# A graph network on one core: both RGCN tables made in one block, tiles posted by ACT, fewer waits and shorter register rows on TensorE, and the clone rows made inside the first dense product

## The chip, the core and the metric

The kernel runs on one core of a Trainium2 chip. The metric is the device time of one execution in microseconds, the median of several. The engines are named as in the profile: PE (TensorE; its weight loads are PEld), DVE (VectorE), ACT (ScalarE), POOL (GpSimd) and SP (SyncE). A trailing q (PEldq, POOLq, SPq) means the sequencer of an engine: register loads, semaphore posts, branches and the issue of DMAs.

## The reference

There are N = 3125 nodes with 128 features and 50,000 edges (src, dst), sorted by dst; each edge has one of R = 9 types. Four graph layers follow each other, each with a residual and a layer norm:

```
x = layernorm(x + ARMA(x))        # two stacks of 3, dense products with D^-1/2 A D^-1/2
x = layernorm(x + GCN(x))
x = layernorm(x + RGCN(x))        # two layers, below
x = layernorm(x + sum over edges of x[src] @ W_neigh.T + b + x @ W_self.T + b)
```

The RGCN, which matters here, has in each of its two layers 18 weights and biases (9 types, two directions) and one for the node itself. With cnt[s] the number of edges of kind s at a node (at least 1):

```
hidden = output @ W[-1] + b[-1]
for r in range(R):
    for inv in (0, 1):
        s = r + R * inv
        msum = agg[s] @ W[s] + count[s] * b[s]     # agg[s]: sum of output over edges of kind s
        hidden = 2.0 * (hidden + msum) / cnt[s]
```

Unrolled, every edge adds to its node one row, output[other end] @ W[s] + b[s], times a factor that depends on the node and the kind; the own row has a factor as well.

## The kernel before

The nodes are NT = 25 tiles of P = 128. The program is a row of stages. Each stage opens a block in which every engine has its own instruction list, and a barrier of all engines stands between two blocks (in the profile the lines L801, L1447, L1549 and the like are such boundaries). The order of work inside a block is written out by hand, with semaphores.

Stages, in order of time: loading, sorting of the edges by either end and counting (to 645 us); `heavy_stage`, which finds nodes of unusually many edges ("clones": a node's second row) and the list `k.need`; `staircase_stage` and `pair_counts_stage`, which make the dense matrix of edge counts (`pairs`, 25 tiles of 128 x 3200 in fp16, and `exact` in uint16) and end at 895 us; `clone_rows_stage` (L1544), to 910; the first dense product `sum_x` in `dense_stage`; the ARMA layers; GCN; and then, for each RGCN layer, two table stages, the sum and a turn back; at last the neighbour layer.

**`clone_rows_stage`.** POOL gathers 128 rows of `exact` and 128 of `pairs` (L1560, L1561), DVE subtracts (L1566), SP stores the difference behind the last real rows of `pairs` (L1571): counts that don't fit fp16 go in two parts.

**`dense_stage`.** SP streams tiles of `pairs` through a ring of four (L1652). DVE, ACT split the features in bf16 parts (L1745, L1777, L1780), PE multiplies (L1694), 21 matmuls a tile. `beside` is other work that DVE does behind its splits; `loads` are weights for later that SP issues between tiles. POOL copies rows out (L1628).

**`table_stage`.** For a layer it makes first `by_src`, then `by_dst`: for every node and type the row output @ W[s] + b[s], 9 x 128 floats, in DRAM. ACT copies a tile of the transposed features into `fed` (L878), PE does three 128x384 products of it (L869; PSUM banks in a ring of J = 5), DVE adds the bias and drains each (L895), SP stores the tile (L935) from a ring of five. SP also waits for stores: `landed(t - BACK)` with BACK = 2 posts tile t - 2 into `tiled` (L929), after it has issued the store of tile t. POOL waits in `behind` for `tiled` to reach `needs[n]` (L2558) and gathers the first BEHIND = 48 rows lists (L2546: 128 edges each, one indirect DMA of 128 rows of 512 bytes) into the ring `got` of PLACES = 128. `needs` is in integer registers from `k.need`, computed in `heavy_stage` as the row number times 1/1152 plus 1.01, rounded, at most NT. In the second table stage POOL gathers 56 more, up to EARLY = 104, and PE and DVE make the own row of each node, in seven groups of four tiles (L827, L837, L841).

**`typed_sum_stage`.** It works in steps of U = 16 items. An item is 128 edges of one order and one node tile: POOL has gathered the 128 rows (L2099; a POOL wait for `ps_sum_rgcn L2180` means that the ring is full), SP posts landed groups of four (L2080), DVE has made a 128 x 128 selection `select` with the edges' factors (L2255), and PE multiplies the two into the PSUM slot of the node tile (L2180). There are C = 416 items an order, 832 a layer, so 52 steps. In layer 0 the factors are found on the way (`find`): for later steps PE also turns one-hots (L2108 `flip`) and looks up the factors (L2115 `look`), DVE copies (L2232), chooses (L2236 to L2248), closes the selection (L2255) and makes the next one-hot (L2227, which posts `heated`). For each half step (OCTET = 8 items) the PE sequencer loads 8 x 4 registers from `k.ring` (L2155): PSUM slot, `freed` count, place in `got`, `landed` count; in layer 0 it also loads 8 of `look_at` (L2123). At the top of a step it waits for `heated` and `selected`. ACT empties and seeds PSUM slots (L2218, L2203), reading where a tile ends from five-register loads (L2211).

Of the kernel before, what the change touches and what calls it, by code (L numbers as in the profile page):

```python
# [16 lines left out]
P = 128  # L17
# [761 lines left out]
BACK = 2  # L779


def piece(first, width, terms, bias=None, target=None):

    return first, width, terms, bias, target


def table_stage(nc, k, tag, pieces, tables, width, scale=None, gathers=None, behind=None, own=None):  # L790
# [10 lines left out]
    with Stage(nc, tag) as c:  # L801
# [8 lines left out]
        if own is not None:  # L810
            own_weights, own_xT, own_bias, own_factor, own_acc = own
            ps_own = c.psum("ps_own", [P, 8 - J, 512])
            own_multiplied, own_biased, own_scaled = c.sems("own_multiplied", "own_biased", "own_scaled")
        FOURS = -(-NT // 4)

        def four(g):

            return slice(4 * g, min(4 * g + 4, NT))

        def own_product():  # L820

            for g in range(FOURS):
                tiles = four(g)
                if g >= 8 - J:
                    nc.tensor.wait_ge(own_biased, g - (8 - J) + 1)
                for t in range(tiles.start, tiles.stop):
                    last = nc.tensor.matmul(ps_own[:, g % (8 - J), t % 4 * P:t % 4 * P + P], own_xT[:, t * P:t * P + P],  # L827
                                            own_weights, start=True, stop=True)
                last.then_inc(own_multiplied, 1)

        def own_sum():

            for g in range(FOURS):
                tiles = four(g)
                n = tiles.stop - tiles.start
                nc.vector.wait_ge(own_multiplied, g + 1)
                nc.vector.tensor_tensor(own_acc[:, tiles, :],  # L837
                                        ps_own[:, g % (8 - J), 0:n * P].rearrange("p (t f) -> p t f", f=P),
                                        own_bias[:, None, :].to_broadcast([P, n, P]), ALU.add).then_inc(own_biased, 1)
                nc.vector.wait_ge(own_biased, g + 1)  # L840
                nc.vector.tensor_tensor(own_acc[:, tiles, :], own_acc[:, tiles, :],  # L841
                                        own_factor[:, tiles, None].to_broadcast([P, n, P]), ALU.mult).then_inc(own_scaled, 1)

        if gathers is not None:
            @block.gpsimd
            def _(gp):
                gathers(gp)

        if behind is not None:
            (tiled,) = c.sems("tiled")  # L850

            @block.gpsimd
            def _(gp):
                behind(gp, tiled)

        @block.tensor
        def _(pe):
            nc.tensor.sem_inc(multiplied, M * J)
            if own is not None:
                own_product()  # L860
            with pe.Fori(0, TURNS) as i:
                for m in range(M * J):
                    j, (first, w, terms, bias, target) = m // M, pieces[m % M]
# [9 lines left out]
        def feed(engine, copy):  # L873
            with engine.Fori(0, TURNS) as i:
                for j in range(J):
                    engine.wait_ge(multiplied, i * (M * J) + M * j + M)
                    for q, turned in enumerate(feeds):
                        copy(fed[:, j, q, :], turned[:, bass.ds((i * J + j) * P, P)]).then_inc(copied, 1)  # L878

        def drain_turn(engine, i, first_turn):  # L880
            for m in range(M * J):
                j, (first, w, terms, bias, target) = m // M, pieces[m % M]
                if m % M == 0 and not first_turn:
# [1778 lines left out]
```

## Time and profile before

| what | value |
|---|---|
| time, median of 3 runs | 4873.02 us (4870.8 to 4875.13) |
| profiled execution | 4878.79 us, span 4877.5 us |
| granted TensorE clock, mean | 0.796 of full speed |
| adjacency to the end of the clone rows | 645 to 909.9 us |
| first dense product | 910 to 1025 us |
| tables, layer 0 and 1 | 2647 to 2802 us, 3699 to 3855 us |
| sum, layer 0 and 1 | 2802 to 3694 us, 3855 to 4706 us |

The span is the time from the first to the last instruction in the profile. Times in all views are counted from the start of the span. A timeline row gives the start, the duration (of a run of like instructions, from the first start to the last end), the engine, the line of the kernel, the instruction and its count, and in brackets how long the engine had been idle and what released it; "issue" there means that nothing shown in the profile held it.

### The profile page before, as it was taken

How to read it: one execution, taken by the hardware profiler on the slowest of the kernel's cores; microseconds unless marked ns; L12 is line 12 of the kernel's file. 1: busy time of each engine (PE TensorE's matmuls, PEld its weight loads, DVE VectorE, ACT ScalarE, POOL GpSimd, SP SyncE). 2: the span in 40 equal slices, each digit the busy share in tenths (PEclk: the TensorE clock that was granted, in tenths of full speed). 3: DMA queues.
4: the chain of work that ended last, by engine and by line, in shares of the span. 5: the costliest groups of instructions: out<-in, count | busy, mean ns of one | idle time of the engine just before them, and what ended most of it. 6: DMA issues, size and time to landing. Idle time of an engine off the chain costs nothing. (4 is left out here: it accounts for less than half of the span.)

```text
span 4877.5 us, 63370 instructions
## 1 busy us (share of the span) xinstructions
PE 3725.2 (76%) x16872; PEld 2405.0 (49%) x16874; DVE 2430.0 (50%) x3836; ACT 955.7 (20%) x2715; POOL 2043.5 (42%) x2229
## 2 busy tenths in 40 slices
PE   5977966698999979999989567676676665444459
PEld 2544522356555535555555356566564454333345
DVE  7988989405888861111235544444444633222221
ACT  2946838323000031111121000000001000000011
POOL 0000011103776611011101667777774777777740
PEclk7988979899999989999989755656667765555569
DMA  3000015715888817446544522222224422222224
GB/s 139 0 0 0 0 68 202 224 64 207 293 293 291 292 63 239 143 167 221 181 149 161 213 66 52 53 53 53 52 53 152 171 53 53 52 53 53 52 69 165
DMA packets 168584, 593.25 MB, mean 122 GB/s; under 512 B 47569, under 2 KB 59442, under 8 KB 168061
## 3 DMA queue, kind: packets, MB, share of 16 engines
q0 software_dynamic: 97200, 308.78, 20.7%
q1 hardware_dynamic: 70854, 282.16, 16.3%
q8 instruction: 69, 1.13, 0.1%
q14 instruction: 71, 0.57, 0.0%
q10 hardware_dynamic: 390, 0.60, 0.0%
HBM read 445.10 MB, written 146.27 MB: 121 GB/s over the span
## 5 line engine op out<-in xcount | busy, mean ns | idle before, releaser
L2180 PE MATMUL ps_sum_rgcn<-gathered_rgcn,select_sum_rgcn 128*128 x3328 | 1010.3, 450 | 446.1 <-SPq L2080 241.9
L2180 PEld LDWEIGHTS ps_sum_rgcn<-gathered_rgcn,select_sum_rgcn 128*128 128x128 f32 x3328 | 787.3, 306 | 525.5 <-issue 519.0
L2099 POOL DMA_INDIRECT gathered_rgcn<-by_dst,row x782 | 737.8, 944 | 238.3 <-issue 226.4
L2099 POOL DMA_INDIRECT gathered_rgcn<-by_src,row x574 | 541.6, 944 | 203.4 <-issue 160.6
L726 PE MATMUL ps_sum_arma<-gathered_sum_arma,select_sum_arma 128*128 128x384 f32 x1664 | 553.3, 492 | 20.3 <-DMA gathered_sum_arma<-arma,other 18.1
L712 POOL DMA_INDIRECT gathered_sum_arma<-arma,other x416 | 393.4, 946 | 382.3 <-POOLq L801 211.9
L1694 PE MATMUL ps_sum_arma<-pair_counts_sum_arma,parts_sum_arma 128*128 128x448 f16 x2625 | 519.5, 354 | 5.3 <-DMA pair_counts_sum_arma<-pairs 5.3
L726 PEld LDWEIGHTS ps_sum_arma<-gathered_sum_arma,select_sum_arma 128*128 128x128 f32 x1664 | 308.3, 191 | 265.1 <-issue 61.5
L760 DVE TENSOR_TENSOR acc_arma_end<-acc_arma_end,ps_sum_arma 128x768 f32 x416 | 396.9, 954 | 58.6 <-PE ps_sum_arma L726 36.2
L2108 PE MATMUL ps_turn_sum_rgcn<-ident,one_hot_sum_rgcn 128*128 128x128 bf16 x832 | 243.9, 301 | 232.8 <-issue 198.3
L2255 DVE TENSOR_TENSOR select_sum_rgcn<-one_hot_sum_rgcn,ps_coef_sum_rgcn 128x2048 f32<-128x2048 bf16 x52 | 119.0, 2288 | 584.3 <-PE ps_sum_rgcn L2180 584.2
L1694 PEld LDWEIGHTS ps_sum_arma<-pair_counts_sum_arma,parts_sum_arma 128*128 128x128 bf16 x2625 | 257.5, 98 | 226.7 <-DMA pair_counts_sum_arma<-pairs 5.8
L2218 ACT COPY acc_rgcn<-ps_sum_rgcn 128x128 f32<-128x128 f32 x100 | 26.5, 265 | 1686.2 <-PE ps_sum_rgcn L2180 1686.2
L497 PE MATMUL ps_sort<-chunk_one_hot_sort,high_one_hot_sort 128*128 128x416 f16 (+1 forms) x816 | 284.7, 349 | 57.1 <-DVE group_one_hot_sort L455 57.1
L1628 POOL DMA_DIRECT2D rows<-parts_sum_arma x125 | 67.6, 541 | 601.1 <-DVE parts_sum_arma L1780 590.7
L482 ACT ACTIVATE low_one_hot_sort<-place_one_hot_sort,low_in_sort 128x128 f16<-128x128 f16 (+1 forms) x816 | 299.1, 425 | 97.8 <-DVE place_one_hot_sort L455 97.7
L2232 DVE COPY turned_sum_rgcn<-ps_turn_sum_rgcn 128x1024 bf16<-128x1024 bf16 x104 | 71.5, 688 | 437.0 <-PE ps_got_sum_rgcn L2115 411.2
L501 PE MATMUL ps_sort<-chunk_one_hot_sort,low_one_hot_sort 128*128 128x416 f16 (+1 forms) x816 | 283.1, 347 | 0.0
L2546 POOL DMA_INDIRECT gathered_rgcn<-by_src,row x208 | 199.1, 957 | 179.3 <-SPq L929 110.2
L1777 DVE SCALAR_TENSOR_TENSOR rest_sum_arma<-ps_sum_arma,dinv,parts_sum_arma 128x128 f32<-128x128 f32 x125 | 43.8, 350 | 435.3 <-ACT parts_sum_arma L1745 435.3
L2108 PEld LDWEIGHTS ps_turn_sum_rgcn<-ident,one_hot_sum_rgcn 128*128 128x128 bf16 x832 | 114.8, 140 | 257.3 <-issue 213.5
L2227 DVE TENSOR_TENSOR one_hot_sum_rgcn<-local,ps_iota_sum_rgcn 128x2048 bf16<-128x2048 f32 x104 | 237.4, 2284 | 7.5 <-DVE select_sum_rgcn L2255 1.8
(459 smaller groups left out, 5321.2 us busy)
## 6 DMA issues: line engine op xcount, KB each, us to landing
pair_counts_sum_arma<-pairs SPq DMA_DIRECT2D x125, 800.0 KB, 4.4
by_src<-rows_rgcn_src_table SPq DMA_DIRECT2D x50, 576.0 KB, 3.4
by_dst<-rows_rgcn_dst_table SPq DMA_DIRECT2D x50, 576.0 KB, 3.8
exact<-whole_pairs SPq DMA_DIRECT2D x25, 800.0 KB, 3.4
pairs<-whole_pairs POOLq DMA_DIRECT2D x25, 800.0 KB, 5.3
pair_counts_sum_x<-pairs SPq DMA_DIRECT2D x25, 800.0 KB, 4.5
pair_counts_sum_gcn<-pairs SPq DMA_DIRECT2D x25, 800.0 KB, 4.5
air_counts_sum_neighbour<-pairs SPq DMA_DIRECT2D x25, 800.0 KB, 4.4
```

Of the source, the lines that this page charges most:

```text
L482: nc.scalar.activation(self.low[e, parity, u // 2, :, u % 2], place, ACT.Copy, scale=o.low_in[e, bass.ds(i * U + u, 1)]).then_inc(self.wei ...
L497: nc.tensor.matmul(self.ps[:, 0, 0:C], self.high[e, parity, pair, :, at], chunk, start=False, stop=False)
L501: nc.tensor.matmul(self.ps[:, 1, 0:C], self.low[e, parity, pair, :, at], chunk, start=False, stop=False)
L712: nc.gpsimd.indirect_dma_start(got[:, n % PLACES, :], None, table, bass.IndirectOffsetOnAxis(ap=rows[:, n:n + 1], axis=0)).then_inc(arrive ...
L726: last = nc.tensor.matmul(ps[:, (u % RING) * BANKS + b, 0:W], select[:, u, :], got[:, u % PLACES, b * W:b * W + W], start=True, stop=True)
L760: nc.vector.tensor_tensor(row.rearrange("p a (b w) -> p (a b) w", w=W), row.rearrange("p a (b w) -> p (a b) w", w=W), part, ALU.add).then_ ...
L1694: return nc.tensor.matmul(ps[:, g, 0:here.stop - here.start], parts[:, n % HOLD, part * P:part * P + P], count[:, n % RING, here], start=s ...
L2099: nc.gpsimd.indirect_dma_start(got[:, n % PLACES, :], None, table, bass.IndirectOffsetOnAxis(ap=o.row[:, n % C:n % C + 1], axis=0)).then_i ...
L2108: inst = nc.tensor.transpose(ps_turn[:, half, v, :], hot[:, parity, half * OCTET + v, :], k.ident16[:, :])
L2180: nc.tensor.matmul(ps[:, bass.ds(slot, P)], select[:, parity, u, :], rows[:, bass.ds(place, D)], start=False, stop=False, skip_group_check ...
L2227: nc.vector.tensor_tensor(hot[:, parity, :, :], k.local[:, bass.ds(first, U), None].to_broadcast([P, U, P]), ps_iota[:, None, 0:P].to_broa ...
L2546: nc.gpsimd.indirect_dma_start(got[:, n, :], None, typed[0], bass.IndirectOffsetOnAxis(ap=k.orders[0].row[:, n:n + 1], axis=0)).then_inc(k ...
```

## The change

**Tables.** `typed_tables_stage` takes the place of both table stages of an RGCN layer. One block makes the 50 tiles of both tables. PE reads the features where they are, without `fed`; it and DVE do the own groups every third tile after the first table. ACT, otherwise idle, waits for each store of the first table and posts `tiled`; SP only issues stores. POOL gathers 48 row lists behind `needs` and, once all 25 tiles are there, 56 more. `table_stage` stays for the ARMA table alone, with the branches that no caller uses any more taken out.

**`k.need`** is now exact: row // 128 * 7282 >> 16, plus 1, in int32.

**Register rows.** A row of `k.ring` holds, for eight items, 8 x (slot, place), two `landed` counts and four `freed` counts: RING_ROW = 22. PE waits for `landed` once in four items, for all four, and for `freed` once in two.

**Clone rows.** `clone_rows_stage` is gone. In `sum_x` POOL issues its two gathers first, DVE subtracts after its 25 splits and before `beside`, SP stores the difference before it issues tile CLONED = 9 and waits for it to land before it issues the last tile.

**Ends.** The list of block ends on ACT in `pair_counts_stage` is uint16 and read without a mask.

```
@@ typed_tables_stage (new; rgcn_layer calls it once per layer)
+            needs = nc.values_load_multi_w_load_instructions(
+                k.need[0:1, 0:U], engines=(mybir.EngineType.Pool,), min_val=1, max_val=NT, ...)[1]
+            for n in range(U):
+                gp.wait_ge(tiled, (needs[n] & COUNTS))
+                nc.gpsimd.nop(nofuse=True)
+                for lane in range(LANES):
+                    gather(lane * U + n)
+            gp.wait_ge(tiled, NT)
+            for n in range(BEHIND, EARLY):
+                gather(n)
...
+            for v in range(TILES):
+                order, t = divmod(v, NT)
+                for part in range(M):
+                    m = v * M + part
+                    s = order * R + part * PARTS
+                    if m >= J:
+                        pe.wait_ge(drained, m - J + 1)
+                    nc.tensor.matmul(ps[:, m % J, 0:W], xT[:, t * P:t * P + P],
+                                     w[:, s:s + PARTS, :].rearrange("p s g -> p (s g)"), start=True,
+                                     stop=True).then_inc(multiplied, 1)
+                g = own_at(v)
...
+            for v in range(TILES):
+                order, t = divmod(v, NT)
+                if v >= J:
+                    dve.wait_ge(stored[v % J], 16 * (v // J))
...
+            for t in range(NT):
+                act.wait_ge(stored[t % J], 16 * (t // J + 1))
+                nc.scalar.sem_inc(tiled, 1)
...
+            for v in range(TILES):
+                order, t = divmod(v, NT)
+                sp.wait_ge(drained, M * v + M)
+                sp.dma_start(tables[order][t * P:t * P + P, :], rows[:, v % J, :]).then_inc(stored[v % J], 16)
@@ heavy_stage
-            then(nc.vector.tensor_scalar(tiles[:, :], ps[0:1, 3, P:P + U], 1.0 / (R * P), 1.01, ALU.mult, ALU.add))
-            nc.vector.tensor_scalar_min(k.need[0:1, :], tiles[:, :], float(NT))
+            then(nc.vector.tensor_copy(tiles[:, :], ps[0:1, 3, P:P + U]))
+            then(nc.vector.tensor_single_scalar(tiles[:, :], tiles[:, :], 7, ALU.arith_shift_right))
+            then(nc.vector.tensor_scalar(tiles[:, :], tiles[:, :], 7282.0, None, ALU.mult))
+            then(nc.vector.tensor_single_scalar(tiles[:, :], tiles[:, :], 16, ALU.arith_shift_right))
+            nc.vector.tensor_scalar(k.need[0:1, :], tiles[:, :], 1.0, None, ALU.add)
@@ pair_counts_stage
-                    act.wait_ge(multiplied, (ends[g] & COUNTS)
-                                if i * SPANS + g < BLOCKS_OF_PAIRS - 1 else ITEMS + V)
+                    act.wait_ge(multiplied, ends[g] if i * SPANS + g < BLOCKS_OF_PAIRS - 1 else ITEMS + V)
@@ dense_stage, sum_x only (exact is not None)
+                nc.gpsimd.indirect_dma_start(clone_whole[:, :], None, exact[:, :], at).then_inc(k.cloned, 16)
+                nc.gpsimd.indirect_dma_start(clone_half[:, :], None, pairs[:, :], at).then_inc(k.cloned, 16)
...
+                if exact is not None and n == CLONED:
+                    sp.wait_ge(clone_made, 1)
+                    sp.dma_start(pairs[NP - P + LAST:NP, :], clone_rest[LAST:P, :]).then_inc(clone_stored, 16)
+                if exact is not None and n == NT - 1:
+                    sp.wait_ge(clone_stored, 16)
...
+                dve.wait_ge(k.cloned, 32)
+                nc.vector.tensor_tensor(clone_rest[:, :], clone_whole[:, :], clone_half[:, :],
+                                        ALU.subtract).then_inc(clone_made, 1)
@@ typed_sum_stage, step of PE
-                            k.ring[0:1, bass.ds(first + u, OCTET), :].rearrange("p c a -> p (c a)"), engines=(PE,),
+                            ring_rows[0:1, bass.ds((s * 2 + half) * RING_ROW, RING_ROW)], engines=(PE,),
...
-                    pe.wait_ge(landed, (ring[4 * v + 3] & COUNTS))
+                    if v % GROUP == 0:
+                        pe.wait_ge(landed, (ring[2 * OCTET + v // GROUP] & COUNTS))
+                    if v % SLOTS == 0:
+                        pe.wait_ge(freed, (ring[2 * OCTET + OCTET // GROUP + v // SLOTS] & COUNTS))
+                        nc.tensor.nop(nofuse=True)
...
-                    pe.wait_ge(freed, (ring[4 * v + 1] & COUNTS))
-                    nc.tensor.nop(nofuse=True)
@@ rgcn's storage
-            k.ring = late.sb("ring", [P, 2 * C, 4], I32)
+            k.ring = late.sb("ring", [P, 2 * C // OCTET, RING_ROW], I32)
```

## Rows read from the trace of the kernel before

**Rows 1.** The page of the profiled run: busy time and share of the span.
```profile
PE 3725.2 (76%) x16872; PEld 2405.0 (49%) x16874; DVE 2430.0 (50%) x3836; ACT 955.7 (20%) x2715; POOL 2043.5 (42%) x2229
```

**Rows 2.** Windows of both sums: us, PE, PEld, DVE, ACT, POOL, clock, DMA, GB/s.
```profile
2802.00:3694.00 892.00, 626.27 (x3330) 535.92 (x3330) 411.63 (x418) 26.41 (x100) 639.74 (x678) 0.59 0.20 53
3855.00:4707.00 852.00, 434.73 (x1666) 367.94 (x1666) 234.50 (x108) 26.64 (x100) 639.72 (x678) 0.54 0.21 52
```

**Rows 3.** Waits of TensorE, layer 0 and then layer 1: total us, times, longest.
```profile
PE ps_sum_rgcn L2180 <- SPq L2080: 1.7, 7, 0.3
...
PE ps_sum_rgcn L2180 <- SPq L2080: 240.2, 113, 3.1
```

**Rows 4.** Timeline (start, us, instruction, idle before) at the ends of both RGCN sums.
```profile
3665.83 0.94 POOL L2099 DMA_INDIRECT gathered_rgcn<-by_dst,row  x1 [0.30 <-issue]
...
3690.05 3.82 PE L2180 MATMUL ps_sum_rgcn<-gathered_rgcn,select_sum_rgcn 128*128 x16 [1.82 <-issue]
...
4700.58 0.94 POOL L2099 DMA_INDIRECT gathered_rgcn<-by_dst,row  x1 [0.30 <-issue]
...
4702.26 3.94 PE L2180 MATMUL ps_sum_rgcn<-gathered_rgcn,select_sum_rgcn 128*128 x16 [1.82 <-issue]
```

**Rows 5.** Timeline of one step of layer 0's sum.
```profile
3623.35 0.29 PE L2108 MATMUL ps_turn_sum_rgcn<-ident,one_hot_sum_rgcn 128*128 128x128 bf16 x1 [2.62 <-issue]
...
3634.94 2.29 DVE L2227 TENSOR_TENSOR one_hot_sum_rgcn<-local,ps_iota_sum_rgcn 128x2048 bf16<-128x2048 f32 x1
...
3640.12 0.27 PE L2108 MATMUL ps_turn_sum_rgcn<-ident,one_hot_sum_rgcn 128*128 128x128 bf16 x1 [2.41 <-issue]
```

**Rows 6.** Lines that load registers on TensorE: ns min/median/max, first and last start.
```profile
L2155 PEldq TENSOR_LOAD <-ring_late x208: 2127/2132/2142, 2818.9 to 4699.7; - x104
...
L2123 PEldq TENSOR_LOAD <-look_at_late x104: 586/589/599, 2808.2 to 3670.7; - x104
...
L1463 PEldq TENSOR_LOAD <-item_at_adjacency x48: 1102/1553/3272, 679.0 to 881.0; - x48
```

**Rows 7.** Timeline of POOL in the table stages of layer 0.
```profile
2661.44 0.98 POOL L2546 DMA_INDIRECT gathered_rgcn<-by_src,row  x1 [59.49 <-SPq L929]
...
2725.97 0.94 POOL L2546 DMA_INDIRECT gathered_rgcn<-by_src,row  x1 [4.87 <-POOLq L801]
```

**Rows 8.** The line that posts stored tiles, from 2640 to 2661.3.
```profile
L929 SPq EVENT_SEMAPHORE  x4: 17/17/17, 2654.8 to 2660.6; - x4
```

**Rows 9.** The tile the drains write and SP stores, over the whole trace.
```profile
L935 SPq DMA_DIRECT2D by_src<-rows_rgcn_src_table x50: 319/320/320, 2650.7 to 3750.3; - x50
...
DMA to landing us min/median/max: 2.7/3.4/4.0
```

**Rows 10.** Timelines of the table stages of layer 0, VectorE and POOL.
```profile
2648.73 48.29 DVE L895 TENSOR_TENSOR rows_rgcn_src_table<-ps_rgcn_src_table,typed_bias_late 128x384 f32<-128x384 f32 x75 [1.92 <-PE ps_rgcn_src_table L869]
...
2728.33 0.69 DVE L841 TENSOR_TENSOR acc_rgcn<-acc_rgcn,factor 128x512 f32<-128x512 f32 x1
...
2728.45 1.39 POOL L2546 DMA_INDIRECT gathered_rgcn<-by_src,row  x1 [0.30 <-issue]
```

**Rows 11.** Timeline of POOL at the start of layer 0's sum.
```profile
2850.69 0.94 POOL L2099 DMA_INDIRECT gathered_rgcn<-by_src,row  x1 [18.36 <-PE ps_sum_rgcn L2180]
```

**Rows 12.** The lines of the two block boundaries around the clone rows.
```profile
L1447 PEldq EVENT_SEMAPHORE  x1: 51/51/51, 895.2 to 895.2; - x1
...
L1549 PEldq EVENT_SEMAPHORE  x1: 51/51/51, 909.9 to 909.9; - x1
```

**Rows 13.** A window over the start of the first dense product.
```profile
915.00:950.00 35.00, 33.39 (x168) 16.66 (x165) 24.38 (x75) 12.17 (x41) 11.60 (x22) 0.95 1.08 275
```

**Rows 14.** Timeline of TensorE in the first dense product.
```profile
953.87 70.33 PE L1694 MATMUL ps_sum_x<-pair_counts_sum_x,parts_sum_x 128*128 128x448 f16 x357 [5.48 <-DMA pair_counts_sum_x<-pairs]
```

**Rows 15.** Timeline of VectorE in the heavy-node stage.
```profile
645.08 0.16 DVE L1259 COPY clone_node_heavy<-ps_heavy 128x2 f32<-128x2 f32 x1 [0.64 <-PE ps_heavy L1273]
```

**Rows 16.** The line in which ACT loads five registers.
```profile
L2211 ACTq TENSOR_LOAD <-ends x20: 541/1117/1137, 2802.7 to 4619.3; - x20
```

More of the change, by code:

```diff
@@ L771, in _, with table_stage @@
             turn(TURNS_OF_CHUNKS - 1, True)
[L779 to L790, printed above, removed]
+def table_stage(nc, k, tag, pieces, tables, width, scale):
     M = len(pieces)
@@ L808, in table_stage @@
         block = c.block()
[L810 to L854, printed above, removed]
         @block.tensor
@@ L880, in drain_turn @@
[L880 to L883, printed above, removed]
-                    engine.wait_ge(stored[j], i * 16 * len(tables))
-                engine.wait_ge(multiplied, i * (M * J) + m + 1 + M * J)
-                if scale is not None:
-                    nc.scalar.nop(nofuse=True)
-                to = rows[:, j, first:first + w] if target is None else \
-                    target[:, bass.ds(i * J + j, 1), 0:w].rearrange("p a f -> p (a f)")
-                if scale is not None:
-                    last = nc.scalar.activation(to, ps[:, m % J, 0:w], ACT.Copy, scale=scale[:, bass.ds(i * J + j, 1)])
-                elif bias is None:
-                    last = nc.vector.tensor_copy(to, ps[:, m % J, 0:w])
-                else:
-                    last = nc.vector.tensor_tensor(to, ps[:, m % J, 0:w], bias, ALU.add)
-                last.then_inc(drained, 1)
@@ L898, in drain @@
[L898 to L921 removed]
+                        nc.vector.tensor_copy(fed[:, j, q, :], turned[:, bass.ds((i * J + j) * P, P)]).then_inc(copied, 1)
@@ new lines, in _, with turn @@
+        @block.scalar
+        def _(act):
+            def turn(i, first_turn):
+                for m in range(M * J):
+                    j, (first, w, terms) = m // M, pieces[m % M]
+                    if m % M == 0 and not first_turn:
+                        act.wait_ge(stored[j], i * 16 * len(tables))
+                    act.wait_ge(multiplied, i * (M * J) + m + 1 + M * J)
+                    nc.scalar.nop(nofuse=True)
+                    nc.scalar.activation(rows[:, j, first:first + w], ps[:, m % J, 0:w], ACT.Copy,
+                                         scale=scale[:, bass.ds(i * J + j, 1)]).then_inc(drained, 1)
+            nc.scalar.sem_inc(drained, J)
+            turn(0, True)
+            with act.Fori(1, TURNS) as i:
+                turn(i, False)
@@ L923, in _ @@
         @block.sync
         def _(sp):
-            if behind is not None:
-                def landed(t):
-                    sp.wait_ge(stored[t % J], 16 * (t // J + 1))
-                    nc.sync.sem_inc(tiled, 1)
-                ((table, first, w),) = tables
-                sp.wait_ge(k.filled, 16)
-                for t in range(NT):
-                    sp.wait_ge(drained, M * t + M + J)
-                    sp.dma_start(table[t * P:t * P + P, :], rows[:, t % J, first:first + w]).then_inc(stored[t % J], 16)
-                    if t >= BACK:
-                        landed(t - BACK)
-                for t in range(NT - BACK, NT):
-                    landed(t)
-                return
@@ L2146, in step @@
                 s, parity = i * TURN + at, at % 2
-                first = after(i, at, 0)
                 near, far = after(i, at, 1) if find else None, after(i, at, 2) if find else None
```

198 lines of the change are left out of this document (106 added, 92 removed).

## The prediction

> **What bounds the kernel now.** I read the share of busy time first and laid it aside: TensorE is busy 76% over the span [rows 1], which mixes stages with different limits. The change touches four places, so I asked for the windows of each, then for the waits in them. In the two RGCN sums GpSimd (POOL) issues 678 gathers in 640 us in either layer, while TensorE's busy time differs by 190 us [rows 2]: layer 1 runs at POOL's pace. TensorE's waits for a landed gather confirm it: 240.2 us in 113 waits in layer 1, 1.7 us in 7 in layer 0 [rows 3]. Layer 0 is another matter: its last gather ends at 3665.83 + 0.94 = 3666.77, and TensorE's last item at 3693.87, 27.1 later; in layer 1 the same distance is 4706.20 - 4701.52 = 4.68 [rows 4]. (A gather there takes 0.94 and the next begins 0.30 later: 1.24 to 1.25 each.) So layer 0 ends with the TensorE/VectorE loop. One step of that loop (16 items) is 3640.12 - 3623.35 = 16.77 us. It goes round so: TensorE does the first eight items, VectorE copies what they turned, makes the next selection and ends with the one-hot at 3634.94 + 2.29 = 3637.23, and only then does TensorE's sequencer load the registers of the next step; its array begins 2.89 later [rows 5]. That gap is a 32-register load (2.13) and an 8-register load (0.59) [rows 6], plus 0.17.
>
> **The tables (twice).** Before a layer's sum, TensorE makes both tables while POOL already gathers 48 rows, passes a block boundary, gathers 56 more and passes another. In layer 0 the gathers run from 2661.44, with a break of 4.87 at the inner boundary [rows 7]. The first break goes: 4.87 - 0.30 = 4.6. The outer one stays. The start moves too: the first gather waits for four posted tiles; SP posts tile 3 only after it has issued the store of tile 5, the fourth post is at 2660.6 [rows 8]. With ACT posting at landing, and the exact integer count (three tiles are enough for the first rows where the rounded formula said four), the third store, issued about 2654.5 (the first at 2650.67 plus two steps of 1.93), lands 3.4 later [rows 9] at 2657.9, and the gather follows by the same 0.8: 2658.8, so 2.65 earlier. No ACT copy ahead of the first product: 0.4 more. Per layer 7.65, and 15.3 for two. If the count still asks for four in this data, the start gains 1.1: then 6.1 a layer, 12; if neither start term comes, 9. Upper bound 17, with the whole 4.87 and a landing of 2.7, the least seen, in both layers. What else the new block does is covered: 150 drains of 0.644 (48.29 for 75) and 14 instructions of 0.69 for the seven own groups are 106 us on VectorE [rows 10], beside 104 gathers of 1.25 and the 11.4 before the first, 141 on POOL. If that cover were gone nothing would be left to gain. Where VectorE's own sum meets a gather, the gather is slower, 1.39 for 0.94 [rows 10]; the seven meetings are now spread out, the same seven: nothing. The drains ran beside gathers before as well.
>
> **Fewer waits and a shorter register row in the sums.** TensorE's four registers an item become 2.75: 22 for eight items rather than 32. Durations before: 8 registers 0.59, 16 at least 1.10, 32 in 2.13 [rows 6], so 0.53 for each eight with a small start. I take 22 as 24: 1.62, that is 0.51 to 0.52 less, for the half load that is exposed; the other half's load lies beside VectorE's chain. 52 steps give 26 to 27. The waits themselves (three small sequencer instructions an item) hide beneath 0.75 us an item of array time. The gain is cut off by POOL: its last gather can end only as much earlier as its one long wait does, 18.36 us for item 28 at 2850.69 [rows 11], two exposed loads earlier, 1.1: 3665.7. From there TensorE needs 4.68 less one shorter load, 4.2: 3669.9 for 3693.87, a gain of 24.0. Bounds: 0 if the load is hidden after all, 27 without the cut, and below nothing if a short row is a bad one (below). Layer 1 is POOL's; only the last load shows, 0.5. Half 1's load is not at issue unless it grows by over a microsecond.
>
> By the Trainium skill ("TensorE: Matmul & The Clock Gate", the section on the array as 32x32 sub-arrays) TensorE's queue holds 64 instructions, against 8 of other engines. Read as a rule for this loop, the sequencer runs far ahead and a load costs the array nothing; the sum would be without the 24.0. The row at 3640.12 speaks against it: the load stands behind a wait on VectorE, so the queue has drained.
>
> **Clone rows.** The stage of its own lasts from one barrier (895.2) to the next (909.9) [rows 12]: 14.7 gone. Its two gathers (800 KB each) now share the first microseconds of the dense product with the streamed tiles, where the DMA engines are full already: share 1.08 and 275 GB/s in its first 35 us [rows 13]. 1.64 MB at 275 GB/s are 6.0 us. How much TensorE feels, no row shows. Bounds 0 (TensorE waits for VectorE's splits first, and then does 168 matmuls at its own pace) and 6.0. I take 2.8, near half: 1.2 before the first tile, the rest at the wait of 5.48 for streamed data at 953.87 [rows 14]. So 11.9. The subtraction stands behind VectorE's 25 splits, which run at TensorE's first products and are done long before tile 9; SP stores the result before it issues that tile, and were it late, tiles 9 on would be, which TensorE reads 40 us into the stage. POOL's row copies queue behind the two gathers, late by two gathers (2.5), and nothing in this stage reads them.
>
> **At nothing.** Three more small VectorE instructions for the count (0.16 each) hide partly in the 0.64 wait beside them [rows 15]; if not, 0.5. The rewritten lists lie beside the GCN product, where TensorE sets the end. The masks off ACT's sequencer in the pair counts save nothing, because VectorE bounds that stage.
>
> **The sum** is made against the profiled run: 4878.8 (span 4877.5 and 1.3 around it); the median is 5.8 under it, and I take the difference off the median. 15.3 + 24.0 + 0.5 + 11.9 = 51.7: 4873.0 - 51.7 = 4821.3 us.
>
> **The rivals.**
> 1. The sequencer's load is hidden, or another wait ends at the same time, so that the sums gain nothing. For it: half 1's load is hidden already, so the sequencer does run ahead where nothing stops it. Against it: the sum 2.13 + 0.59 + 0.17 fits the gap to 0.01. Gain 27.7 - 0.5: 4845.8.
> 2. Rows of 88 bytes cost more at every other step. The five-register loads of ACT, at 20-byte spacing, took 0.541 at least and 1.117 in the median [rows 16]: a start that isn't a multiple of 16 bytes seems to double a load. Half 0's rows start at multiples of 176 bytes, which 16 divides, and are exempt; if the grain is 32 bytes, every other one isn't, and pays a fourth piece of 0.53. Gain 14 in place of 24: 4831.
> 3. The clone gathers delay the first product by all that their stage took, since they come ahead of the streamed tiles and POOL's copies: no gain there, 4833.
> 4. The other side: the short row doubles the exposed load at every step, as five-register rows double [rows 16]. 22 registers in six pieces of 0.53 are 3.2, 1.07 more than now, and 52 of them cost 56, with nothing to cut it off: 4873.0 - 27.7 + 56 = 4901. It decides from an exposed load of about 2.65 (2.13 + 27.7/52), where all other gains are eaten. For it: the spread of 0.54 to 1.14 in that row. Against it: the 176-byte start.
>
> **Chances.** The forecast 0.66, rival 1 0.12, rival 2 0.10, rival 3 0.05, rival 4 0.05, and 0.02 for a load of about 2.65, which is no change. Between 4811 (bounds 17, 27, 0.5 and 14.7 give 4814, and some for the spread of the runs) and 4847 lie the forecast and the first three rivals, most of 0.93; I stop there, since what is outside is rival 4. The forecast's own range is 4812 to 4830. A measurement of this kernel can tell about 0.2%, 10 us, from no change: faster 0.92, same 0.03, slower 0.05.
>
> **What would show it.** In the new tables block no break on POOL but at its end, and the first gather some 11.4 us after the last stage's end, or 13 with four tiles. TensorE's ring load at 1.6, the step at 16.2, TensorE waiting for landed gathers at the end of layer 0, and ending 4.2 after the last gather. In the dense product the start 14.7 earlier, the first tile's product late by about 1, no wait of SP before tile 9. Wrong it would be if the ring load were 2.1 or more, if TensorE's start in a step hung on something behind the load, or if the dense product's first tiles were starved.

## The result and the profile after

The changed kernel took 4848.1 us (median of 7 runs, 4840.3 to 4860.2) against 4873.0 before (7 runs, 4868.0 to 4875.1): ratio 0.9950, interval 0.9938 to 0.9962. The forecast was 4821.3 in 4811 to 4847. The sign was right, the size was not: 25 us came and 52 were forecast. A second timing gave 4838.3 against 4871.0 (0.9934, 0.9917 to 0.9950). The profiled run before (4878.8) and after (4848.1) differ by 30.7; the table splits that, in microseconds. Each row begins where an engine starts the next part; all are differences of rows in the timelines.

| part | before | after | difference | forecast |
|---|---|---|---|---|
| start to the barrier after the pair counts | 895.0 | 898.3 | +3.3 | 0 |
| to the end of the first dense product, clone rows included | 129.2 | 120.3 | -8.9 | -11.9 |
| ARMA, GCN, norms (and the ACT copy ahead of layer 0's first table product) | 1623.6 | 1621.6 | -2.0 | -0.4 |
| layer 0, first table product to the sum's first matmul | 154.5 | 151.3 | -3.2 | -7.2 |
| layer 0, sum, to the first matmul of the turn back | 892.2 | 875.2 | -17.0 | -24.0 |
| layer 1, turn back and tables | 160.6 | 156.8 | -3.8 | -7.7 |
| layer 1, sum | 855.8 | 856.3 | +0.5 | -0.5 |
| rest | 166.6 | 167.0 | +0.4 | 0 |

Five terms are short. The rows that tell why follow, first POOL's timeline from the tables into layer 0's sum, of the changed kernel, which answers to [rows 7] and [rows 11]:

```profile
2650.45 0.97 POOL L884 DMA_INDIRECT gathered_rgcn<-by_src,row  x1 [55.54 <-ACTq L950]
...
2791.90 0.94 POOL L2119 DMA_INDIRECT gathered_rgcn<-by_src,row  x1 [9.44 <-POOLq L862]
...
2841.06 0.94 POOL L2119 DMA_INDIRECT gathered_rgcn<-by_src,row  x1 [19.49 <-PE ps_sum_rgcn L2201]
```

The start is as forecast and a little better: the first table product is at 2640.21, so the first gather follows 10.2 later, where it was 13.7 (in layer 1, 10.3 where it was 15.3). The inner break is gone. But the outer one has grown. Before, its row in the same view read:

```profile
2802.67 0.94 POOL L2099 DMA_INDIRECT gathered_rgcn<-by_src,row  x1 [5.51 <-POOLq L801]
```

Two breaks of 4.87 and 5.51 became one of 9.44. The lines of the boundary say whose it is (duration in ns, then first and last start):

```profile
L862 PEldq DRAIN  x2: 2553/2554/2555, 2740.3 to 3772.3; - x2
L862 DVEq DRAIN  x2: 590/591/592, 2742.8 to 3774.9; - x2
...
L862 SPq DRAIN  x2: 7/7/7, 2747.3 to 3779.4; - x2
L862 POOLq DRAIN  x2: 23501/23506/23511, 2767.5 to 3799.5; - x2
```

TensorE, VectorE and SP are at the barrier by 2747.3; POOL's drain ends at 2767.5 + 23.5 = 2791.0, 8.6 after its last gather (2781.51 + 0.94). The barrier at the end of a sum, in the changed kernel and then before:

```profile
L2071 POOLq DRAIN  x2: 24076/24082/24089, 3642.4 to 4655.1; - x2
...
L2071 PEldq DRAIN  x2: 2153/2153/2153, 3663.5 to 4676.3; - x2
```
```profile
L2051 POOLq DRAIN  x2: 24074/24074/24074, 3651.8 to 4686.6; - x2
...
L2051 PEldq DRAIN  x2: 812/814/817, 3693.1 to 4705.4; - x2
```

In layer 1 POOL's drain ended at 4710.7 before, 9.1 after its last gather, while TensorE was done at 4706.2: the distance of 4.68 that the prediction took from [rows 4] was not what ended that stage. In layer 0 the drain (3675.9) stood far before TensorE's end at 3693.9. Now it ends at 3666.5, 0.9 after TensorE:

```profile
3656.38 0.95 POOL L2119 DMA_INDIRECT gathered_rgcn<-by_dst,row  x1 [0.30 <-issue]
...
3661.80 3.78 PE L2201 MATMUL ps_sum_rgcn<-gathered_rgcn,select_sum_rgcn 128*128 x16 [5.15 <-issue]
```

The register loads, which answer to [rows 6]:

```profile
L2174 PEldq TENSOR_LOAD <-ring_late x208: 1842/3538/5239, 2808.2 to 4668.9; - x104
...
L1478 ACTq TENSOR_LOAD <-end_of_adjacency x25: 1917/2257/3084, 678.7 to 882.5; - x25
```

The load of 22 registers takes 1.84 at one half and 5.24 at the other; the eight 16-bit ends on ACT take 2.26, where eight 32-bit ones took 0.55 in the median. TensorE in the first dense product, in answer to [rows 14]:

```profile
903.70 26.24 PE L1691 MATMUL ps_sum_x<-pair_counts_sum_x,parts_sum_x 128*128 128x448 f16 x126 [12.17 <-DMA pair_counts_sum_x<-pairs]
931.03 4.13 PE L1691 MATMUL ps_sum_x<-pair_counts_sum_x,parts_sum_x 128*128 128x448 f16 x21 [1.09 <-DMA pair_counts_sum_x<-pairs]
939.33 5.70 PE L1691 MATMUL ps_sum_x<-pair_counts_sum_x,parts_sum_x 128*128 128x448 f16 x21 [4.17 <-DMA pair_counts_sum_x<-pairs]
949.55 69.07 PE L1691 MATMUL ps_sum_x<-pair_counts_sum_x,parts_sum_x 128*128 128x448 f16 x357 [4.51 <-DMA pair_counts_sum_x<-pairs]
```

One wait of 5.48 has become three, 9.8 together, and the first tile's product comes 5.2 after the barrier in place of 4.6.

### The profile page after: what moved, and what is told of

Read it like the earlier page. It is cut to its first block and busy times, and to the rows that moved or that the text cites. A ratio compares the mean times of both kernels' runs of the same rounds, so it can differ in the third digit from the quotient of the medians.

```text
span 4846.8 us, 59076 instructions
## 1 busy us (share of the span) xinstructions
PE 3669.6 (76%) x16873; PEld 2375.3 (49%) x16874; DVE 2428.9 (50%) x3839; ACT 928.6 (19%) x2615; POOL 2041.1 (42%) x2229
## 5 line engine op out<-in xcount | busy, mean ns | idle before, releaser
L2201 PE MATMUL ps_sum_rgcn<-gathered_rgcn,select_sum_rgcn 128*128 x3328 | 961.1, 438 | 499.0 <-issue 272.8
L2201 PEld LDWEIGHTS ps_sum_rgcn<-gathered_rgcn,select_sum_rgcn 128*128 128x128 f32 x3328 | 761.1, 309 | 555.5 <-issue 554.7
```

Of the source, the lines that this page charges most:

```text
L2201: nc.tensor.matmul(ps[:, bass.ds(slot, P)], select[:, parity, u, :], rows[:, bass.ds(place, D)], start=False, stop=False, skip_group_check ...
```

## The experiments

From these rows I formed three theories. **W**: a register load takes four 32-bit registers at a time (0.27 us) where its address is a multiple of 16 bytes, else one at a time (0.24): 5 x 0.27 + 2 x 0.24 = 1.83 for the 1.84, and 22 x 0.24 = 5.3 for the 5.24. **P**: both layers now end with POOL, its last gather and the drain behind it; a boundary breaks the gathers for 0.93 us plus 0.082 for each gather of its block (48: 4.87, 56: 5.51, 104: 9.44), with a limit, since 678 give no more than 9.1 to the drain's end. **S** against **T**: the dense product loses its 6 us to SP's queue, or to the bytes.

**Group 1** ran at a time when every execution took about 5500 us, that of before too (5555.5 median). Its times compare only among each other, and its traces with the others only up to the dense product. My expectations for the next group put this down to gathers that land late. The trace of `after_again` says otherwise: POOL's last gather of layer 1 ended at 5239.0, and SP had posted the last landed group of four by 5241.8, while TensorE worked on until 5322.0.

```profile
L2100 SPq EVENT_SEMAPHORE  x7: 3/17/698, 5240.8 to 5241.8; - x7
```

TensorE was behind there, after pauses of up to 8 us between its products that no row explains; the tables took 203 us where they take 151 otherwise. What slowed these executions is not known.

`after_again`: the changed kernel, no edit.

> The changed kernel once more, as the yardstick of this group. If its spread (4840 to 4860 in seven runs) comes from the first dense product, where transfers collide, the trace differs there by some us from the first one, and nowhere else by over 2.

Measured 5497.3, ratio 0.9894 (0.9865 to 0.9923). The pair counts' barrier came at 893.8, not 898.3, with the same 16-bit ends. Where the spread comes from can't be read in a group so slow; `after_third`, below, answers it.

`row24`:

```
+RING_USED = 2 * OCTET + OCTET // GROUP + OCTET // SLOTS
-RING_ROW = 2 * OCTET + OCTET // GROUP + OCTET // SLOTS
+RING_ROW = 24
-        freed = ring[:, :, 2 * OCTET + OCTET // GROUP:RING_ROW]
+        freed = ring[:, :, 2 * OCTET + OCTET // GROUP:RING_USED]
+        nc.vector.memset(ring[:, :, RING_USED:RING_ROW], 0)
```

> The register rows are padded from 22 to 24 integers (88 to 96 bytes), so that each begins at a multiple of 16 bytes. Theory W (a load goes four registers at a time, 0.27 us, where its address is a multiple of 16 bytes, and else one register at a time, 0.24): all ring loads 1.60 us, in place of 1.84 and 5.24 by turns. Rival to W (the 5.24 is contention with VectorE beside it): the load of half 1 stays above 3. Theory P (layer 0 now ends with POOL's last gather and the 9.1 us of its drain, so that a faster TensorE loop is worth nothing): only the wait of POOL for a full ring shrinks, from 19.5 to about 17.5: 2 us less than the changed kernel. Rival to P (the loop of TensorE and VectorE still sets layer 0's end): steps 0.4 shorter, 52 of them, 15 to 21 us less.

Measured 5428.7, ratio 0.9769 (0.9742 to 0.9795): 69 less than `after_again`. TensorE ends both layers in this group, so that its loads show: from the sum's first matmul to the next stage's, layer 0 took 17.6 less and layer 1 47.8 less. Over its last steps of layer 1 TensorE took some 11.6 us for 16 items in `after_again`, with 5.1 idle ahead of the eight items whose load takes 5.24, and 7.6 in `row24`:

```profile
5306.92 3.68 PE L2201 MATMUL ps_sum_rgcn<-gathered_rgcn,select_sum_rgcn 128*128 x16 [5.08 <-issue]
5310.91 2.23 PE L2201 MATMUL ps_sum_rgcn<-gathered_rgcn,select_sum_rgcn 128*128 x16 [0.31 <-issue]
```

(The first line is eight items behind the load of 5.24, the second the eight behind the load of 1.84.) No theory here was made for that case.

`ends_i32`:

```
-        q.end_of = c.sb("end_of", [P, NT, SPANS + 1], U16)
+        q.end_of = c.sb("end_of", [P, NT, SPANS + 1], I32)
-                    act.wait_ge(multiplied, ends[g] if i * SPANS + g < BLOCKS_OF_PAIRS - 1 else ITEMS + V)
+                    act.wait_ge(multiplied, (ends[g] & COUNTS)
+                                if i * SPANS + g < BLOCKS_OF_PAIRS - 1 else ITEMS + V)
```

> Only the list of block ends on ACT is 32 bits wide again, and masked as before. Theory W: the eight-register load is 0.54 again in place of 2.26, and the counting stage ends 3.3 us earlier: 3.3 less than the changed kernel. Rival (the 3.3 came from something else in that stage, such as chance in its transfers): no change.

Measured 5488.9, ratio 0.9875 (0.9844 to 0.9906). The load is as W has it, but the stage's barrier at 894.7 was no earlier than that of `after_again`:

```profile
L1478 ACTq TENSOR_LOAD <-end_of_adjacency x25: 543/548/765, 678.1 to 879.1; - x25
```

Over all traces the stage lasts from its first matmul to this barrier 213.6 to 219.9 with 16-bit ends (11 traces, mean 217.2) and 211.6 to 216.5 with 32-bit ones (5, mean 215.2). The spread of one kind is as large as the +3.3 of the table, so most of that may be chance; that the longer load costs 2 us of it stays open.

`clone_late`:

```
-    CLONED = 9
+    CLONED = 16
```

> CLONED = 16 in place of 9: SP stores the difference seven tiles later. Theory S (what starves TensorE in the first dense product is SP's queue: the store's issue, 5.7 us, stands ahead of tile 9 while SP is behind already): the waits for tiles 8 to 10, 1.1 + 4.2 + 4.5, shrink to about 5.5 in all, 4 us less than the changed kernel. Rival T (it is the bytes of the two gathers and the store that the queues must carry): the first product still takes 121 us, 0 to 1.5 less.

Measured 5496.5, ratio 0.9896 (0.9870 to 0.9922). S falls: from the barrier to the product's end it took 120.1, as in the changed kernel (120.3), and the waits only moved:

```profile
930.94 4.13 PE L1691 MATMUL ps_sum_x<-pair_counts_sum_x,parts_sum_x 128*128 128x448 f16 x21 [1.10 <-DMA pair_counts_sum_x<-pairs]
937.51 4.13 PE L1691 MATMUL ps_sum_x<-pair_counts_sum_x,parts_sum_x 128*128 128x448 f16 x21 [2.43 <-DMA pair_counts_sum_x<-pairs]
948.85 69.48 PE L1691 MATMUL ps_sum_x<-pair_counts_sum_x,parts_sum_x 128*128 128x448 f16 x357 [7.20 <-DMA pair_counts_sum_x<-pairs]
```

**Group 2** ran at the speed of the first timing (before: 4870.9). The record names the same chip number, 12, for groups 1 and 2, so the chip that the next expectation blames for the slow group is not shown to be the reason.

`row24_again`: the kernel of `row24`.

> The 24-integer rows once more, since the first group ran on a chip whose gathers land late (before took 5555 us there). On a chip like that of the first timing: theory P (POOL and its drain end layer 0) 2 us less than the changed kernel, 4846; the rival (the TensorE loop ends it) 15 to 21 less.

Measured 4839.6, ratio 0.9937 (0.9921 to 0.9954). W holds: the other half's load is short as well.

```profile
L2176 PEldq TENSOR_LOAD <-ring_late x208: 1613/1618/1637, 2794.7 to 4651.6; - x104
```

P holds for this kernel. The regular steps, from one of VectorE's 52 selections to the next (two lengths make up most of them), are 16.73 and 16.64, where the changed kernel has 16.97 and 16.88 and before had 17.25 and 17.14; yet layer 0's sum took 871.7, 3.5 less than in the first trace of the changed kernel (7.3 less than in `after_third`, below), not 15 to 21. From the first selection to the last, 51 steps, pass 838.7, where the changed kernel has 843.1 and 850.0 in two traces and before 864.8. TensorE ends at 3646.1 and waits for a barrier at 3649.4. The ring-full wait shrank by 3.3:

```profile
2824.22 0.94 POOL L2121 DMA_INDIRECT gathered_rgcn<-by_src,row  x1 [16.23 <-PE ps_sum_rgcn L2203]
```

`early84`:

```
-EARLY = BEHIND + 14 * GROUP
+EARLY = BEHIND + 9 * GROUP
```

> EARLY is BEHIND + 9 groups: 84 gathers in the tables block in place of 104, 20 more in the sum. Theory P, with the law read from three boundaries (from the last gather of a block to the next gather pass 0.93 us and 0.082 for each gather of the block, up to some 9.4): the break at the boundary is 7.8 in place of 9.4. The sum's block then starts 26 us earlier, and POOL's wait of 19.5 for a full ring in layer 0 is gone, as 44 more gathers (55 us) reach to item 28. Layer 0 ends 21 us earlier, layer 1 1.6: 22 to 23 less than the changed kernel. Rival (the break is the same for any number, set by code loading or the like): 20 less, break 9.4. Rival (the early gathers are needed, TensorE starves at the start of a sum): 0 or slower.

Measured 4824.5, ratio 0.9899 (0.9880 to 0.9917), 23.6 less than the changed kernel's 4848.1 (and 13.8 less than its second timing, 4838.3). Layer 0 (tables and sum) took 1005.5 for 1026.5 (1030.3 in `after_third`), layer 1 1011.4 for 1013.1 (1011.3): some 21 to 25 us, nearly all in layer 0. The break is the one that the law gives, and no ring-full wait follows:

```profile
2763.30 0.94 POOL L2119 DMA_INDIRECT gathered_rgcn<-by_src,row  x1 [7.81 <-POOLq L862]
```

`two_blocks`:

```
-            typed_tables_stage(nc, k, f"rgcn_tables{layer}", xT, [dram["by_src"], dram["by_dst"]], got, acc)
+            for half in (0, 1):
+                typed_tables_stage(nc, k, f"rgcn_tables{layer}{half}", xT, [dram["by_src"], dram["by_dst"]], got, acc, half)
...
-    TILES = len(tables) * NT
+    TILES = NT
...
+            if half:
+                for n in range(BEHIND, EARLY):
+                    gather(n)
+                return
...
-                order, t = divmod(v, NT)
+                order, t = half, v
```

> The tables block is split in two again, by_src with its 48 gathers and by_dst with 56, all else as changed. Theory P: breaks of 4.9 and 5.5 in place of 0.3 and 9.4, so 0.7 slower in each layer, 1.4 in all, if POOL bounds both. Rival M (the step of the prediction: one boundary less is worth 4.6 a layer): 9 slower.

Measured 4843.1, ratio 0.9940 (0.9924 to 0.9957). That lies between the two timings of the merged block (4848.1 and 4838.3), so the total can't tell 1.4 from 9; the trace can. Its breaks are 4.87 and 5.51 again. From the first table product to the sum's first matmul passed 152.2 in layer 0 and 151.2 in layer 1, where the merged block has 151.3 in both. So the merge is worth 0.9 us in layer 0 and nothing in layer 1, and M, the prediction's step, falls.

```profile
2710.92 0.94 POOL L884 DMA_INDIRECT gathered_rgcn<-by_src,row  x1 [4.87 <-POOLq L862]
...
2788.78 0.94 POOL L2120 DMA_INDIRECT gathered_rgcn<-by_src,row  x1 [5.51 <-POOLq L862]
```

`clone_stage`:

```
         pair_counts_stage(nc, k, q, dram["exact"], dram["pairs"])
+    clone_rows_stage(nc, k, dram["exact"], dram["pairs"])
...
-                        beside=beside, exact=dram["exact"])
+                        beside=beside)
```

> The clone rows have their own stage again (14.7 us), all else as changed. Theory T (their bytes cost the first dense product 6 us): 8.7 slower than the changed kernel. The prediction's figure: 11.9 slower. The product itself from barrier to barrier 115 in place of 121.

Measured 4844.7, ratio 0.9952 (0.9936 to 0.9967). The total shows nothing, as other stages differed by more. From the counts' barrier to the product's end it took 128.1 (before 129.2; changed kernel 120.3 and 122.3, 119.1 in `row24_again`): T holds in that the 6 us go with the transfers, and the move is worth some 8 of the 14.7. Over all traces, the three with a stage of its own took 128.2 in the mean and the 13 without 120.2, so the move gave 8.0 and the transfers cost 6.7. The store's 0.48 MB (75 rows of 6400 bytes), which the 1.64 MB of the prediction leave out, would be 1.7 at its 275 GB/s, 7.7 with the gathers. Whether it is the bytes or the number of packets was not tested. Both waits are those of before again:

```profile
913.24 34.30 PE L1723 MATMUL ps_sum_x<-pair_counts_sum_x,parts_sum_x 128*128 128x448 f16 x168 [26.31 <-DMA pair_counts_sum_x<-pairs]
952.88 68.91 PE L1723 MATMUL ps_sum_x<-pair_counts_sum_x,parts_sum_x 128*128 128x448 f16 x357 [5.34 <-DMA pair_counts_sum_x<-pairs]
```

**Group 3** (before: 4871.0).

`after_third`: the changed kernel.

> The changed kernel once more, the yardstick of this group: 4848 with a spread of some 8 to either side, its counting stage ending between 893.7 and 898.5 (by now seen at both, with 16-bit and with 32-bit ends), layer 0 ending with POOL's drain.

Measured 4838.3, ratio 0.9934 (0.9917 to 0.9950). Barrier at 895.2; layer 0's sum 879.0, at the end of which TensorE (3660.0) and POOL's drain (3656.0) were 4 apart: the two are near a tie in this kernel, and either may come last. With 22-integer rows and 104 early gathers POOL's drain came last in `after` (by 0.9), TensorE in `after_third`, `two_blocks` (by 3.6) and `clone_stage` (by 0.4). So P is right for layer 1; in layer 0 it is a tie until the loads are shorter. And the spread doesn't come from the first dense product: that took 122.2 for 120.3, while the untouched stages up to the tables took 8.7 less than in the first trace and layer 0's sum 3.8 more.

`row32`: `row24`'s edit, but

```
+RING_ROW = 32
```

> The fewer waits of TensorE alone: the rows are padded to 32 integers, as long as before. If the load alone made a step shorter (the prediction's step, and theory P): loads 2.13, regular steps of 17.25 and 17.14 between two selections again (changed kernel 16.97 and 16.88, before 17.25 and 17.14), the TensorE loop ends layer 0 about 14 us later than with the changed rows, less 1 that POOL's end was later: 11 to 13 slower than the changed kernel. Rival (the waits and their sequencer instructions were on the path too): steps of 16.9, no slower than the changed kernel.

Measured 4854.2, ratio 0.9968 (0.9955 to 0.9980), 15.9 slower than `after_third`; 9.3 of that lies in layer 0's sum, 6.1 in the stages between dense product and tables, which the edit doesn't touch. Loads 2.13, regular steps 17.25 and 17.15, 864.4 for the 51 (before 864.8): the waits that were dropped are worth nothing in a step, all of the step's gain is the load's. The sum of layer 0 took 888.3, 3.9 less than before; 3.6 of that lies behind the last selection (11.4 for 15.0). The changed kernel took 16.6 there in `after_third`: its load of 5.24 gives that back and more.

`before_early84`: `early84`'s edit, on the kernel before.

> The kernel before with 84 early gathers in place of 104, in two blocks as it was. Theory P: the second table's block is then ended by TensorE, VectorE and SP (2791.8, 10 earlier than 2801.9), not by POOL. Layer 0, which the TensorE loop ends, gains those 10; in layer 1, which POOL ends, 20 gathers (25 us) more follow a boundary only 10 earlier: 15 later. Together 5 slower than before. Rival (fewer early gathers help whatever the blocks are): 15 to 22 faster than before.

Measured 4876.7, ratio 1.0013 (1.0003 to 1.0022). Layer 0 10.1 faster, layer 1 13.8 slower, against 10 and 15 expected. In two blocks the second table is too long for 36 gathers, and POOL stands idle, though its drain had ended 3.7 after the last gather (4.1 in layer 1):

```profile
2790.03 0.94 POOL L2099 DMA_INDIRECT gathered_rgcn<-by_src,row  x1 [19.53 <-POOLq L801]
```

`best`: `early84`, `row24` and `ends_i32` together.

> The changed kernel with 84 early gathers, 24-integer rows and 32-bit ends. Theory P: layers as with 84 early gathers alone, since POOL and its drain end both and no ring-full wait is left for shorter loads to shorten: 22 to 25 less than the changed kernel, 4822 to 4826, and 46 to 52 less than before. Rival (gains of the parts add up): 30 less than the changed kernel, 4818.

Measured 4820.7, ratio 0.9900 (0.9884 to 0.9917), 17.6 less than `after_third` and 27.4 less than the first timing of the changed kernel. Layer 0 took 1005.6, as with `early84` alone: P again, the parts don't add up: POOL's drain ended 3.2 after TensorE.

**Two single runs** (before 4878.9 beside them).

`pause64`:

```
-EARLY = BEHIND + 14 * GROUP
+EARLY = BEHIND + 4 * GROUP
             for n in range(BEHIND, EARLY):
+                if n == EARLY - GROUP:
+                    gp.wait_ge(drained, M * TILES)
                 gather(n)
```

> 64 early gathers, and POOL waits ahead of the last four until VectorE has drained all 150 products: 60 gathers, a pause of some 18 us, 4 gathers, boundary. Theory Q (what the boundary waits for is a backlog that grows by 0.082 us with each gather issued close behind the last, and runs off in a pause): the break from the last gather to the next is about 1.3 us. Rival N (it goes by the number of gathers since the last boundary): 0.93 + 0.082 x 64 = 6.2.

Measured 4851.3. There was a pause of 16.56 us ahead of the last four gathers, and the break was 6.18 all the same: Q falls, N holds. Group 1 agrees, where the drain behind 104 gathers again ended 8.6 after the last one.

```profile
2739.77 0.94 POOL L884 DMA_INDIRECT gathered_rgcn<-by_src,row  x1 [16.56 <-DVE rows_rgcn_tables L934]
...
2750.64 0.94 POOL L2121 DMA_INDIRECT gathered_rgcn<-by_src,row  x1 [6.18 <-POOLq L862]
```

`best72`: `best`, with

```
-EARLY = BEHIND + 9 * GROUP
+EARLY = BEHIND + 6 * GROUP
```

> The best version with 72 early gathers in place of 84. By the law of the breaks 6.8 in place of 7.8, so 1 us less in each layer, unless TensorE, VectorE and SP, which end 107 us after the block's start, come last: the two should now end within 1 us of each other.

Measured 4819.9. The break was 6.82 in layer 1, as the law has it, and 7.41 in layer 0; the 0.6 there isn't explained, as SP, the last of the others, had reached the barrier 1.4 us before POOL's drain ended (2740.0 and 2741.4). Layer 0 took 1006.5 for 1005.6: one run shows no gain there.

```profile
3755.00 0.95 POOL L2122 DMA_INDIRECT gathered_rgcn<-by_src,row  x1 [6.82 <-POOLq L862]
```

## Why the prediction was off, step by step

The step that failed outright is the inner boundary's; next to it stand three sizes that were off: the load, the end of layer 0 and the cost of the clone rows. Of the 27 us that didn't come, the boundary is 8, layer 0's sum 7 (11 in the second trace), the clone rows 3, and the pair counts 3, which may be chance.

- **The inner boundary: failed.** "The first break goes: 4.87 - 0.30 = 4.6. The outer one stays." The outer one doesn't stay: it took over what the inner one had cost (5.51 became 9.44), as the break goes by the number of gathers since the last boundary. The merge was worth 0.9 in layer 0 and nothing in layer 1 (`two_blocks`), not 4.6 in each: 8.3 of the missing 27.
- **The earlier first gather: right in layer 0**, 3.2 for 3.05, counted from the end of the work before to the first gather (13.8 and 10.6). In layer 1 it came 4.4 earlier, counted from the start of the turn back. The forecast took layer 0's figure for both.
- **The cap on layer 0: right in kind, too low by POOL's drain.** "From there TensorE needs 4.68 less one shorter load, 4.2" read layer 1's end as TensorE's. It was POOL's drain, 9.1 after the last gather. With 3665.7 + 9.1 the stage would end at 3674.8, and so a gain of about 19 follows in place of 24. The changed kernel gained less still, 17.0 in one trace and 13.2 in the other, since with the load as it is TensorE comes as late as the drain; `row24_again`, where the drain does end it, gained 20.5. The last-load term of layer 1, 0.5, was worth nothing for the same reason: TensorE's last items ended 8.3 after the last gather, for 4.7 before, and nothing showed.
- **The load: mechanism right, one size off.** I counted 22 registers as 24. The exposed half took 1.84, not 1.62, for two registers are left over from groups of four. The regular step won 0.27, about 14 over the 52, where 26 to 27 were forecast. "Half 1's load is not at issue unless it grows by over a microsecond": it grew by 3.1. That lengthened the end behind the last selection (16.6 in `after_third`, 11.4 in `row32`), and POOL's ring-full wait near the start was 1.1 longer instead of shorter; with the short loads of `row24` it was 2.1 shorter. `row24` gives what was forecast: 1.62 and 0.51 a step. Rival 4, the doubled load, was the right fear at the wrong half.
- **Rival 1** gave nearly the time measured (4845.8), by luck and not by its mechanism: it had nothing from the sums, and layer 0's sum gained 13 to 17. The load is on the path (`row32`), and the step got shorter by just as much as the load did. What made up the number were the tables and the clone rows, which gave 11 less than it assumed.

By the Trainium skill ("TensorE: Matmul & The Clock Gate", the section on the array as 32x32 sub-arrays), TensorE's queue holds 64 instructions. The runs show that this does not hide the load that stands behind the wait on VectorE: loads of 2.13, 1.84 and 1.62 gave steps of 17.25, 16.97 and 16.73.

- **Clone rows: mis-sized.** The transfers cost the product 6.0 in the profiled pair and 6.7 in the mean of all traces, and not 2.8. The 6.0 of the prediction was no upper bound either, as it left out the store. The place of the store in SP's queue is not to blame (`clone_late`).
- **At nothing:** the count in `heavy_stage` and the lists showed nothing. That the masks off ACT save nothing was right, but the 16-bit load that came with them, at least 3.5 times as long, I hadn't seen.
- **The spread.** The stages between the dense product and the tables, which no edit touches, took 1612 to 1630 us over all traces but those of group 1. That is why one profile against another can't settle terms of a few us by the total, and why the terms above are read stage by stage.

The terms as measured: 7.0 for the tables (forecast 14.9), 17.0 for layer 0's sum (24.0), 8.9 for the clone rows (11.9), 2.0 from the untouched stages, less 3.3 in the pair counts and 0.9 at layer 1's sum and the rest: 30.7 in the profiled pair.

## What to carry to other kernels

Ask of every barrier which engine reached it last, and look for its drain, not only for its last work: a faster engine gains nothing once another one's drain ends the stage. Merging two blocks gives back only what does not depend on their content; here the merge paid by making room for another number, 84 early gathers rather than 104. With it the two RGCN layers gained another 22.7 us, where the change itself had gained 23.5 there; in two blocks the same number lost 3.7 (`before_early84`). And keep rows that a sequencer loads registers from at multiples of 16 bytes, in 32-bit integers and in fours.

## What the runs showed of the hardware

- A block's boundary behind indirect gathers on POOL broke them for 4.87, 5.51, 7.81 and 9.44 us at 48, 56, 84 and 104 gathers, 6.18 at 64 with a pause of 16.6 us ahead of the last four: from 48 to 104 gathers 0.93 us and 0.082 for each one. It went by the count and not by time, and has a limit: counted to the end of POOL's drain it was 8.6 behind 104 and 9.1 behind 678 to 718. Two cases lie off the line: 7.41 at 72 in one layer (6.82 in the other), and a drain of 3.7 and 4.1 behind 36, as long as behind 48 (4.0), where the line has 3.0; there VectorE was still at work. What is being waited for stays open: the gathered rows were there, since in layer 1 of the kernel before TensorE had done the last product with them over 4 us before the drain ended.
- Register loads on TensorE: 8 in 0.59, 22 in 1.84 (row at a multiple of 16 bytes) or 5.24 (8 bytes off), 24 in 1.62, 32 in 2.13; on ACT, 8 of 32 bits in 0.55, 8 of 16 bits in 1.92 at least. These are floors: in the pair counts the load of 16 registers (L1463 in [rows 6], from rows 64 bytes apart) took 1.10 at least, as four fours would, but 1.55 in the median and up to 3.27, and no run tells what lengthened it. The Trainium skill ("DMA: Bandwidth & Descriptors", "Latency and other measured facts") gives a load of this kind a floor of about 600 ns; the rows agree for eight aligned 32-bit registers (0.59 and 0.55). Beyond that floor the address took the load of 22 from 1.84 to 5.24, and 16-bit integers took that of eight from 0.55 to 1.92 or more.
- In one group, all executions were 12 to 14% slower, and TensorE ended both RGCN layers, 83 us after POOL's last gather in layer 1; there the 24-integer rows won 1.2% over the changed kernel, in the other groups no more than the spread. Why that group was slow isn't known; the gathered rows were there (the last landed group was posted 2.8 us after the last gather).
